# Step-size preparation between the units of a state-space scan: other buffers for exponential, one-plus and logarithm, four PSUM banks in the fill, four pieces later, fewer table loads

## The reference, cut to what matters

```
dt = softplus(t_r @ w_dt.T + b_dt)            # 1024 channels; the same with 512 for the context
A  = -exp(A_log)                              # 16 states per channel
for t:  h = exp(dt_t * A) * h + dt_t * B_t * u_t
        y_t = sum over the 16 states of h * C_t;   y = y + u * D
```

## Time and profile before

| | |
|---|---|
| median of 3 runs | 3246.27 us (3241.14 to 3251.11) |
| the profiled execution | 3242.18 us |
| its span, first to last instruction | 3240.4 us |
| mean granted TensorE clock | 0.837 |
| busy share of PE, DVE, ACT, POOL | 74%, 77%, 38%, 32% |
| the twelve units of scans | from about 40 to 2,626 us |

### The profile page before, as it was taken

The page is one execution under the profiler, slowest core; times in us unless marked ns, Lnnn a source line. Parts: engine busy times, 40 slices in busy tenths (PEclk is TensorE's granted clock), DMA queues, the critical chain, the costliest instruction groups (busy, mean ns, idle before and its releaser), DMA issues.

```text
span 3240.4 us, 20396 instructions
## 1 busy us (share of the span) xinstructions
PE 2410.5 (74%) x6316; PEld 1156.1 (36%) x6316; DVE 2482.0 (77%) x1928; ACT 1236.3 (38%) x1970; POOL 1044.1 (32%) x291
## 2 busy tenths in 40 slices
PE   5683121699888875899878866799787858979964
PEld 1241000244344433344434423344444424445532
DVE  5997989899798988897988988996999943121132
ACT  4433242443624535444435434434435413021222
POOL 0343545424345352323344462322353420000000
PEclk7875555799889986899889976899898878979986
DMA  2128000121216650222135630212146621216920
GB/s 89 39 101 230 0 7 0 32 67 49 75 67 190 212 156 7 77 67 67 51 110 188 216 111 13 78 62 63 46 132 199 202 71 70 73 42 207 294 79 13
DMA packets 151772, 312.07 MB, mean 96 GB/s; under 512 B 29872, under 2 KB 47280, under 8 KB 150064
## 3 DMA queue, kind: packets, MB, share of 16 engines
q1 hardware_dynamic: 130864, 261.41, 26.0%
q10 hardware_dynamic: 15680, 32.58, 2.9%
q0 software_dynamic: 5120, 16.78, 1.5%
HBM read 282.40 MB, written 43.78 MB: 101 GB/s over the span
## 4 chain that ended last, share of the span: by engine, by line
PE 35%; DVE 31%; issue 18%; ACT 9%; DMA 4%; POOL 3%; ACTq 0%; SPq 0%; DVEq 0%; POOLq 0%
DVE hb L1413 12%; PE ps L842 6%; PE ps L849 6%; DVE hb L1421 4%; DVE hb L1330 4%; PE ps L713 3%; PE ps L674 3%; DMA ring<-in_w_edn 2%; PE ps L885 2%; PE ps L980 2%; POOL ya L1690 2%; PE ps L776 2%; DVE sm L1274 1%; PE ps L815 1%; DVE hb L1396 1%
## 5 line engine op out<-in xcount | busy, mean ns | idle before, releaser
L1690 POOL TENSOR_TENSOR ya<-ya,hb 128x2048 f32<-128x2048 f32 x188 | 860.0, 4574 | 1371.1 <-DVE hb L1413 1296.5
L1413 DVE TENSOR_TENSOR_SCAN hb<-da,hb 128x2048 f32<-128x2048 f32 x192 | 865.3, 4507 | 7.3 <-ACT da L1020 6.0
L1020 ACT ACTIVATE da<-dl,pk 128x511 f32<-128x511 f32 x768 | 489.4, 710 | 487.0 <-DVE hb L1413 471.3
L1330 DVE TENSOR_TENSOR hb<-du,ps 128x2048 f32<-128x2048 f32 x192 | 435.9, 2270 | 33.1 <-POOL ya L1690 25.2
L1421 DVE TENSOR_TENSOR hb<-hb,ps 128x2048 f32<-128x2048 f32 x192 | 437.6, 2279 | 3.7 <-PE ps L790 2.9
L684 PE MATMUL ps<-bct,sel 64*128 64x512 f32 x192 | 109.6, 571 | 270.0 <-DVE hb L1330 263.4
L713 PE MATMUL ps<-V,ring 128*128 128x512 f32 x512 | 242.7, 627 | 25.7 <-DVE yg L1371 11.0
L674 PE MATMUL ps<-ring,hid 128*128 128x512 f32 x544 | 241.2, 599 | 7.6 <-DVE hid L1456 4.7
L870 PE MATMUL ps<-ring,hid 128*128 128x352 f32 x480 | 195.4, 491 | 20.3 <-ACT X L1199 20.1
L866 PE MATMUL ps<-ring,hid 128*128 128x352 f32 x480 | 199.5, 499 | 14.7 <-DMA ring<-egu 9.1
L790 PE MATMUL ps<-bct,sel 64*128 64x512 f32 x192 | 102.8, 535 | 135.6 <-DVE hb L1421 135.3
(11 more groups left out here) (242 smaller groups left out, 3341.1 us busy)
## 6 DMA issues: line engine op xcount, KB each, us to landing
ring<-egu SPq DMA_DIRECT2D x240, 352.0 KB, 3.7
ring<-in_w_edn SPq DMA_DIRECT2D x72, 512.0 KB, 5.2
ring<-in_w_fgu SPq DMA_DIRECT2D x44, 512.0 KB, 3.7
ring<-in_w_in SPq DMA_DIRECT2D x32, 512.0 KB, 3.6
hid<-xrows SPq DMA_DIRECT2D x60, 256.0 KB, 4.4
yrows<-X ACTq DMA_DIRECT2D x60, 256.0 KB, 4.7
ring<-in_w_egu SPq DMA_DIRECT2D x24, 512.0 KB, 3.3
ring<-in_w_edn SPq DMA_DIRECT2D x60, 192.0 KB, 4.3
```

The lines of the kernel that those rows point to most:

```text
L1020: i = act.activation(dav(n % 2)[:, k, 1:], dl[:, k, 1:], ACT.Exp, scale=Aneg[:, (4 * (u % 3 - 1) if u % 3 else UC) + k, m:m + 1])
L1330: dve.tensor_tensor(hbv(m % NHB), du[:, :, :], wide(ps[:, 5, :], 4), ALU.mult).then_inc(s["dbu"], 1)
L1413: dve.tensor_tensor_scan(hb[:, h, :], da[:, b % 2, :], hb[:, h, :], 0.0, ALU.mult, ALU.add)\
L1690: pool.tensor_tensor(sums, ya[:, :, :], hbv(m % NHB), ALU.add).then_inc(s["acc"], 1)
```

## The change

- Exp is taken in place in `da[0]`, where Abs now writes; one-plus goes to `du`, Ln to `hb[1]`. So Abs and Relu wait for the scan of state 14 and not for POOL; one-plus waits for the last `dbu` (which reads `du`), Ln for POOL's addition of state 13. DVE's first two operations of `dt_c` now read and write `du` and read `hb[1]`.
- Units 0, 1 and 2 use banks 0 to 3 for the four matmuls, which then do not wait for Abs. Units 1 and 2 wait for `folded` before.
- `dt_exp` and ACT's `dt_b` become one task `dt_ex`. Units 0 to 2 have it once for all four blocks, units 3 to 11 once for each block of 512 columns, as a piece that may stand between two `dt_mm`.
- A table is loaded in `dt_ex` only when an ACT task of another kind has come since the last load.
- `plan()` has the new ranks (14 for `dt_mm`), durations and dependences; `dt_b` on POOL may stand before the last addition of the old unit, and the scans no longer come after `fin`. The orders of all engines come out of it anew. The code of the other tasks is as it was.

```diff
--- before.py
+++ after.py
@@ -74,6 +74,16 @@
...
+def parts(q):
+    return 1 if q < 3 else 4
+def logs(q):
+    return sum(parts(i) for i in range(q))
 def span(t, k):
...
@@ -101,12 +111,16 @@
...
         for k in range(4):
-            after = [(("dt_mm", q, k - 1), "act" if q else "pe")] if k else [last, ready, (("sa", first - 2, 0), "act") if q else None]
-            chain(15, ("dt_mm", q, k), [("pe", 0.9), ("act", 1.45)], *after)
-        put(15, ("dt_exp", q, 0), "act", 3.2, (("dt_mm", q, 3), "act"))
-        put(15, ("dt_b", q, 0), "act", 3.9, (("dt_exp", q, 0), "act"), (("sb", first - 2, 0), "pool") if q else None)
-        put(15, ("dt_b", q, 0), "pool", 4.6, (("dt_exp", q, 0), "act"))
-        put(50, ("dt_c", q, 0), "dve", 6.9, (("dt_b", q, 0), "act"), (("dt_b", q, 0), "pool", -2.2), (("sb", first - 1, 0), "dve") if q else None)
+            after = [(("dt_mm", q, k - 1), "act" if q > 2 else "pe")] if k else [ready, last + (-2.2,) if q > 2 else (("folded", 0, 0), "dve") if q else None, (("dt_c", q - 1, 0), "pe") if q else None]
+            put(14, ("dt_mm", q, k), "pe", 0.9, *after)
+            put(14, ("dt_mm", q, k), "act", 1.45, (("dt_mm", q, k), "pe"), (("sa", first - 2, 0), "act") if q else None,
+                (("sa", first - 2, 0), "dve") if q else None)
+        for k in range(parts(q)):
+            put(15, ("dt_ex", q, k), "act", 5.9 if parts(q) == 1 else 2.3, (("dt_mm", q, 3 if parts(q) == 1 else k), "act"),
+                (("dt_ex", q, k - 1), "act") if k else None, (("sb", first - 3, 0), "pool", -3) if q else None, last + (-2.2,) if q else None)
+        put(15, ("dt_b", q, 0), "pool", 4.6, (("dt_ex", q, parts(q) - 1), "act", -3.9 if parts(q) == 1 else -1.5),
+            (("sb", first - 2, 0), "pool") if q else None)
+        put(50, ("dt_c", q, 0), "dve", 6.9, (("dt_ex", q, parts(q) - 1), "act"), (("dt_b", q, 0), "pool", -2.2), (("sb", first - 1, 0), "dve") if q else None)
         put(40, ("dt_c", q, 0), "act", 2.8, (("dt_c", q, 0), "dve", -2.2))
...
@@ -115,8 +129,7 @@
...
             put(91, ("sa", n, 0), "dve", 4.45 + 2.3 * (n == first), back,
-                (("sa", n - 1, 0), "act") if n > first else (("dt_c", q, 0), "act"),
-                (("fin", q - 1, 0), "dve") if q % 3 != 1 and q and n == first else None)
+                (("sa", n - 1, 0), "act") if n > first else (("dt_c", q, 0), "act"))
             if n < first + NST - 1:
...
@@ -124,7 +137,7 @@
...
         put(15, ("skip", q, 0), "act", 2.9, ready, None if q == 0 else
-            (("fin", q - 1, 0), "dve") if q % 3 != 1 else (("sb", first - 1, 0), "pool"), (("dt_exp", q, 0), "act"))
+            (("fin", q - 1, 0), "dve") if q % 3 != 1 else (("sb", first - 1, 0), "pool"), (("dt_ex", q, parts(q) - 1), "act"))
         if q % 3:
...
@@ -768,12 +781,14 @@
...
                                 pe.wait_ge(*of("h_bc", q // 3, 2))
-                            if q:
+                            if q > 2:
                                 pe.wait_ge(s["dbu"], NST * q)
-                        elif q:
+                            if q in (1, 2):
+                                pe.wait_ge(s["set"], 2)
+                        elif q > 2:
                             pe.wait_ge(s["dt_abs"], 4 * q + n)
                         rows, low = (P, tn) if a >= 0 else (RANKB, tnx)
-                        pe.matmul(ps[:, 5 if q else n, :], cur["d"][0:rows, n * P:(n + 1) * P], low[0:rows, :],
+                        pe.matmul(ps[:, 5 if q > 2 else n, :], cur["d"][0:rows, n * P:(n + 1) * P], low[0:rows, :],
                                   start=True, stop=True).then_inc(s["h_dtm"], 1)
...
@@ -1002,7 +1017,7 @@
...
             def _(act):
-                cnt = {"ln": 0, "h_ln": 0}
+                cnt = {"ln": 0, "h_ln": 0, "table": ""}
...
@@ -1034,7 +1049,15 @@
...
                 act.wait_ge(s["set"], 1)
+                def tables():
+                    if cnt["table"] != "exp_ln":
+                        act.preload_act_table_set("natural_log_exp_and_others")
+                    cnt["table"] = "exp_ln"
                 for t, b, n in order["act"]:
+                    if t not in ("dt_mm", "dt_ex", "dt_c", "sa", "skip", "x_load", "c_load", "hx_load", "t_load"):
+                        cnt["table"] = t
                     if b == 0 and t in ("hx_load", "c_load"):
...
@@ -1111,13 +1134,13 @@
...
                         if q and n == 0:
-                            act.wait_ge(s["acc"], NST * q - 2)
+                            act.wait_ge(s["scan"], NST * q - 1)
                             act.wait_ge(s["da"], NST * q)
...
                         act.wait_ge(s["h_dtm"], 4 * q + n + 1)
-                        bank = 5 if q else n
+                        bank = 5 if q > 2 else n
                         act.activation(dl[:, n, :], ps[:, bank, :], ACT.Relu, bias=bias)
-                        act.activation(hbv(1)[:, n, :], ps[:, bank, :], ACT.Abs, bias=bias).then_inc(s["dt_abs"], 1)
+                        act.activation(dav(0)[:, n, :], ps[:, bank, :], ACT.Abs, bias=bias).then_inc(s["dt_abs"], 1)
                     elif t == "skip":
...
@@ -1129,19 +1152,20 @@
...
                         i.then_inc(s["skip"], 1)
-                    elif t == "dt_exp":
-                        act.preload_act_table_set("natural_log_exp_and_others")
-                        act.wait_ge(s["dt_abs"], 4 * b + 4)
-                        act.activation(hb[:, 1, :], hb[:, 1, :], ACT.Exp, scale=-1.0).then_inc(s["dt_exp"], 1)
-                    elif t == "dt_b":
-                        act.wait_ge(s["dt_exp"], b + 1)
-                        if b:
-                            act.wait_ge(s["acc"], NST * b - 1)
-                            act.wait_ge(s["scan"], NST * b - 1)
-                        act.preload_act_table_set("natural_log_exp_and_others")
-                        act.activation(hb[:, 2, :], hb[:, 1, :], ACT.Identity, bias=1.0).then_inc(s["dt_one"], 1)
-                        act.wait_ge(s["dt_one"], b + 1)
-                        act.activation(da[:, 0, :], hb[:, 2, :], ACT.Ln).then_inc(s["dt_log"], 1)
+                    elif t == "dt_ex":
+                        k = slice(0, 4) if parts(b) == 1 else n
+                        v = logs(b) + n + 1
+                        tables()
+                        act.wait_ge(s["dt_abs"], 4 * b + (4 if parts(b) == 1 else n + 1))
+                        act.activation(dav(0)[:, k, :], dav(0)[:, k, :], ACT.Exp, scale=-1.0).then_inc(s["dt_exp"], 1)
+                        act.wait_ge(s["dt_exp"], v)
+                        if b and n == 0:
+                            act.wait_ge(s["dbu"], NST * b)
+                        act.activation(du[:, k, :], dav(0)[:, k, :], ACT.Identity, bias=1.0).then_inc(s["dt_one"], 1)
+                        if b and n == 0:
+                            act.wait_ge(s["acc"], NST * b - 2)
+                        act.wait_ge(s["dt_one"], v)
+                        act.activation(hbv(1)[:, k, :], du[:, k, :], ACT.Ln).then_inc(s["dt_log"], 1)
                     elif t == "dt_c":
...
@@ -1392,13 +1416,14 @@
...
                     elif t == "dt_c":
-                        dve.wait_ge(s["dt_log"], b + 1)
-                        dve.scalar_tensor_tensor(out=hb[:, 2, :], in0=hb[:, 2, :], scalar=-1.0, in1=da[:, 0, :],
+                        dve.wait_ge(s["dt_log"], logs(b + 1))
+                        duf = du[:, :, :].rearrange("p c t -> p (c t)")
+                        dve.scalar_tensor_tensor(out=duf, in0=duf, scalar=-1.0, in1=hb[:, 1, :],
                                                  op0=ALU.add, op1=ALU.subtract).then_inc(s["dt_res"], 1)
...
                         dve.wait_ge(s["dt_sum"], b + 1)
-                        dve.tensor_tensor(dlf, dlf, hb[:, 2, :], ALU.subtract).then_inc(s["dt_res"], 1)
+                        dve.tensor_tensor(dlf, dlf, duf, ALU.subtract).then_inc(s["dt_res"], 1)
                         dve.wait_ge(s["dt_res"], 2 * b + 2)
...
@@ -1671,10 +1696,11 @@
...
                     elif t == "dt_b":
-                        pool.wait_ge(s["dt_exp"], b + 1)
-                        pool.tensor_tensor(dl[:, :, :], dl[:, :, :], hbv(1), ALU.add).then_inc(s["dt_sum"], 1)
+                        pool.wait_ge(s["dt_exp"], logs(b + 1))
+                        pool.tensor_tensor(dl[:, :, :], dl[:, :, :], dav(0), ALU.add).then_inc(s["dt_sum"], 1)
                     elif t == "dt_c":
                         pool.wait_ge(s["dt_res"], 2 * b + 1)
+                        pool.wait_ge(s["dt_sum"], b + 1)
                         pool.memset(da[:, :, :].rearrange("p i (c t) -> p (i c) t", t=TOK)[:, :, 0:1], 0.0)\
```

## The result

The changed kernel is slower: 3256.83 us (median of 8 runs, 3250.2 to 3258.48) against 3242.89 us (8 runs, 3238.15 to 3251.11) for the kernel before, measured beside it. The ratio is 1.004, its 95% interval 1.0027 to 1.0053. The forecast was 3222, between 3196 and 3247. The profiled execution took 3257.96 us, with a span of 3256.1. Two executions lie far outside the rest, 4326 us of the kernel before and 6164 us of one_piece_bank5_old_mm_plan (its profiled one, so that no row of it is read), and are left out of all ratios.

What follows compares the result with a forecast made beforehand. Bound: hand-overs between units, limited by POOL and DVE's shared access, and a second chain ending last. Gains 3.6 + 10.3 + 9 - 2.3 = 20.6 us; 3242.2 - 20.6 = 3221.6, so 3222, range 3196 to 3247.

Steps and rivals of the forecast that it cites:

- The exclusion: POOL's additions and DVE operations on two SBUF tiles block each other; limits the usual hand-over gain to 2.3 us, not 6.9.
- under 40 was asked for: Sign that the forecast holds: DVE's idle time before L1396 falls from 90 to under 40 us.
- mostly fits in that wait: Units 3 to 11: a piece of about 1.9 us fits ScalarE's 2.16 us matmul wait; logarithm 7 to 9 us earlier.
- unit 4 gains 4.8, unit 7 4.0, unit 10 3.3: Hand-over gains: unit 4 lacks `fin`, the last Exp decides unit 7, the last Abs holds unit 10.
- the five exclusive operations: After POOL's last addition, `fin`, L1675, L1396, L1401 and L1405 run in any order, 13.7 us to `du` instead of 16.0.
- The third rival: Pieces cut the other chain's tanh, adding table loads and waiting, 3.2 us per cut; slower, 3260 at 12 cuts; chance 0.1.
- The fill: Unit 1's four matmuls wait for `folded`; about 274 to 277 against L1396 at 276.63, between +3 and -3 us.
- The scans have 75 us to spare: The second chain ends last from the first mixing on; so half of 20.6 us, 10.3, reaches the end.
- The 9 us for ScalarE being free earlier: Units 5, 8 and 11, routed experts: ScalarE free some 7 us earlier, of which three times 3 us counted.
- `fin` behind the sum: Unit 2: POOL's sum L1675 may take the access first, delaying `fin` and the first mixing 4.5 us; at even odds 2.3.
- part of this width: Planner's orders reshuffle in all stages after small time changes; counted only within the forecast's own range, 3197 to 3236.

Runs made afterwards that it cites:

- one_piece_bank5_old_mm_plan: Changed kernel with one piece per unit, before's planner entries for dt's matmuls, Relu and Abs, and bank 5 for units 1 and 2; 3226.63 us, 0.9949.
- changed_hop_016: Changed kernel with the planner's semaphore allowance HOP at 0.16 instead of 0.15; 3258.09 us, 1.005.
- one_piece_fin_first: Changed kernel with one piece, bank 5, before's planner entries for dt's matmuls, and POOL's sum waiting for `fin` in six units; 3227.74 us, 0.9946.
- changed_fin_first: Changed kernel with POOL's sum waiting for `fin` in units 3, 5, 6, 8, 9 and 11; 3250.45 us, 1.003.
- old_code_new_orders: Code of the kernel before (old buffers, waits, banks, two table loads) in the changed plan's program orders; 3272.83 us, 1.0097.
- one_piece_old_mm_plan: Changed kernel with one piece, also in the planner, and before's planner entries for dt's matmuls, Relu and Abs; 3234.45 us, 0.9976.
- changed_old_exp_due: Changed kernel with one planner line set back: the exponential's entry waits for POOL's accumulation before last, as before; 3254.03 us, 1.0027.
- before_hop_016: Kernel before with only the planner's semaphore allowance HOP moved from 0.15 to 0.16, changing only orders; 3227.59 us, 0.9955.

## Why the prediction was wrong

**Right.** In unit 0 the logarithm ends 1.29 us earlier behind the last Abs, the second load and no more; 0.74 of it reaches the first scan, since POOL's sum lengthens the first subtraction from 2.29 to 2.84 us. The exclusion holds: DVE's idle time before the first subtraction fell by half (44.8 us, where under 40 was asked for), and `fin`, L1421 or L1426 was lengthened in units 2 to 11, to between 3.9 and 6.6 us. The Trainium skill, SBUF — State Buffer, section SBUF: two separate sides, says of the shared port pair that each side holds it for a whole instruction; every lengthened DVE operation here ends 2.15 us after POOL's, about its own length of 2.29, so the traces agree. From POOL's last addition to `du` there are 13.5 us in units 3, 5, 9 and 11, as forecast, but 15.8 in unit 4 and not 11 to 12. A piece takes 1.95 us, the last Exp ends 0.7 and the logarithm 2.0 us behind the last Abs.

**The step that failed first: a piece "mostly fits in that wait" of ScalarE, so that the logarithm comes 7 to 9 us earlier, and unit 4 gains 4.8, unit 7 4.0, unit 10 3.3.** The waits of 2.16 us were read in unit 2. In units 5, 8 and 11 they were 0 to 1.7 us, so three pieces did not fit, and no table load was counted in the hand-over. In unit 4 the tail behind the last Abs did shrink by 5 us; the Abs itself came 3 us later (TensorE's next matmul needs the Abs, and the Abs stands behind the piece and its loads), and POOL's sum lost its cover. I had read unit 4 from POOL's last addition (820.08), as if the five exclusive operations were queued from there. They were not: ScalarE's last Abs was later, and in the kernel before the sum lay beside a table load, the one-plus and the logarithm for nothing. Of a hand-over's three bounds I moved one and left out what the sum was hidden behind. As a sum over units 3 to 11 the pieces cost 8.3 us of hand-over in before's orders (289.4 against 281.0): units 5, 8 and 11 lose 13.3, the other six win 5.0. The third rival's mechanism is in this: 21 table loads at the preparation instead of 10, and four more at the other chain's (97 in all, 82 with one piece), 19 us of ScalarE. But they lengthen the hand-over itself, and not only the other chain as the rival had it. In the changed kernel's own orders there are 90 loads, and taking the pieces out (83 loads) wins nothing: there neither pieces nor loads are what costs.

**The fill was taken as 0, between +3 and -3.** It costs 6.8 us in the medians, 3.8 of them in the two hand-overs of the profiles. I compared the last pair only and took 274 to 277 for the subtraction; in the changed kernel the four matmuls start at 269.41, since the stage of the context's B and C follows the folding on TensorE first, and the subtraction starts at 282.6.

**"The scans have 75 us to spare", so half of their gain reaches the end.** This was a misreading of the chain. From the start of `fin` of unit 11 to the first matmul of the last sequence's mixing (L815, now L830) there are 75.5 us before and 74.2 after, and 73.6 to 76.0 in 18 of the 19 profiles read (91.1 in changed_hop_016): the same expert, normalisation and mixing steps follow the last addition each time. It is not slack but a tail of fixed length, and POOL's last additions stood on that chain in the very view. The execution ends 607 to 613 us behind the end of that `fin` in the same 18, so what is won or lost before it is passed on nearly in full: 19.9 us at `fin` of unit 11, 15.7 at the end of the span; 11.0 and 14.1 with one piece and bank 5. And the scans have nothing to spare at unit 10 either, whose inputs hang on the second chain, as the rows above show. The 9 us for ScalarE being free earlier did not come: behind the last scan the logarithm ended 10.6, 2.3 and 7.3 us earlier in units 5, 8 and 11, but the second chain came later and not earlier (the attention mixing of the first sequence by 38 us).

**`fin` behind the sum was taken as 2.3 us at one place.** It happened at unit 3 (603.70, 6.57 us) and also in units 5, 9 and 11, 4.3 us each. Undone, the span is 12 us less and the median 6; in the orders of one_piece_fin_first it is worth nothing. Since the intervals of the two kernels overlap, the 6 us are not shown to be more than noise.

**The orders were "part of this width".** This is the other step that failed. With one piece the new plan costs 20 to 23 us (3256.1 and 3259.4 against 3236.4), with pieces 8 (3256.8 against 3248.7), with the old code 31. All in all, in medians, along one path: the table load -8.0, the buffers and the earlier start -4.8, the fill's banks +6.8, the pieces +12.4, the plan +8.1, together +14.5. That this is near the 13.9 measured is no test, since such steps add up to the whole difference by construction, and their sizes depend on the path: if the plan comes before the pieces, it costs 23.0 and they win 2.5.
What the plan's loss comes from is shown in part. It has a direction: five kernels with `x1` of the second sequence behind scan 99 or 100 lie at 3255 to 3259 (of two more, changed_fin_first is at 3250 and old_code_new_orders at 3273), and one entry set back (one_piece_old_mm_plan) removes all of it, while another, which reshuffles as much, removes nothing. That the plan counts on preparations that are done earlier than the chip does them, and so lets the scans run ahead of the other chain, fits this, the 31 us that the second chain has lost by unit 6, and the waits of units 7 and 10; it is argued and not shown. changed_old_exp_due put the same places back and won 3 us only. With the pieces, then, something else holds it, and that stays open; so does why before_hop_016's gain and that of the code do not add.

**A version that beats both kernels.** Nine kernels here lie under before with their whole interval. Best is the changed kernel's code with one piece and bank 5, in before's orders (3229.5), with its own plan (3226.6) or with HOP 0.16 (3226.4): 13 to 16 us under before. But before_hop_016 reaches 3227.6 with a constant alone.

## What to carry to other kernels

When an operation is cut in pieces to shorten the tail behind its last input, work out three things in one sum: the tail, the delay of the inputs that now stand behind pieces (and their table loads) on the same engine, and what work of another engine lost its cover; in unit 4 they were -5.2, +3.0 and +2.6 us. Read the waits that the pieces are to fill in each place, and not in one. A distance between two chains is slack only if it changes when one of them moves: compare it in two profiles, or follow the chain across it, before a gain is discounted, and look for a wait of the first chain on the second (here unit 10's inputs). Where a planner makes the orders, a change of its entries is an edit of its own: run the new code in the old orders and the old code in the new ones, and redraw the old kernel once (here -14 us by a constant) before the difference is put down to the code.
